# Decoder block on one core: the order of the first four loads, and of the first operations behind them

## The reference

```python
x = x + linear_attention(layernorm(x))       # 16 heads of 16; q, k, v, o projections with biases
x = x + cross(ctx, ctx, masks, layernorm(x)) # see below
x = x + ffn(layernorm(x))                    # Hadamard transforms round gate/up (1024 wide) and down
```

```python
qp = ctx @ Wq.T + bq;  kp = ctx @ Wk.T + bk          # ctx: 4 x 256 x 64
scores = (qp @ kp.T) / 8 * layernorm(x)              # 256 x 256 for each batch
x = x + softmax(where(mask, -inf, scores))
```

## Time and profile before

| | |
|---|---|
| time, median of 3 runs | 125.45 us (125.14, 125.45, 128.5) |
| the profiled execution: its own time | 125.14 us |
| the profiled execution: span from first to last instruction | 123.3 us |
| mean granted clock of TensorE in it | 1.00 of full speed |
| busy share of the span: PE, PEld, DVE, ACT, POOL | 97%, 87%, 67%, 58%, 56% |

### The profile page before, as it was taken

The page is one execution under the profiler, slowest core; times in us unless marked ns, Lnnn a source line. Parts: engine busy times, 40 slices in busy tenths (PEclk is TensorE's granted clock), DMA queues, the critical chain, the costliest instruction groups (busy, mean ns, idle before and its releaser), DMA issues.

```text
span 123.3 us, 2272 instructions
## 1 busy us (share of the span) xinstructions
PE 119.2 (97%) x804; PEld 107.0 (87%) x804; DVE 82.7 (67%) x207; ACT 71.6 (58%) x158; POOL 68.5 (56%) x89
## 2 busy tenths in 40 slices
PE   5999999999999999999999999999999999999990
PEld 2259999999999999999989999988888888889890
DVE  1399989899889899899998959674522332220521
ACT  1785696679748689888491479983135444280000
POOL 2228959979979966959802605762005574066000
DMA  3999910280000000000000110000110000000121
GB/s 123 316 377 423 398 76 5 53 330 3 8 0 0 0 5 3 0 0 0 0 5 0 43 45 0 5 0 0 39 46 3 5 0 0 0 0 0 54 73 43
DMA packets 3823, 7.64 MB, mean 62 GB/s; under 512 B 544, under 2 KB 1952, under 8 KB 3684
## 3 DMA queue, kind: packets, MB, share of 16 engines
q1 hardware_dynamic: 3806, 7.50, 16.8%
q10 hardware_dynamic: 6, 0.01, 0.0%
HBM read 6.46 MB, written 1.05 MB: 61 GB/s over the span
## 4 chain that ended last, share of the span: by engine, by line
PE 97%; POOL 0%; DVE 0%; issue 0%; POOLq 0%
PE bank L1283 19%; PE bank L1295 18%; PE bank L1300 11%; PE bank L1177 10%; PE bank L1304 5%; PE bank L1201 5%; PE bank L1239 5%; PE bank L1155 4%; PE bank L1115 4%; PE bank L1211 3%; PE bank L1221 3%; PE bank L1309 2%; PE bank L1146 2%; PE bank L1247 2%; PE bank L1128 1%; PE bank L1259 1%
## 5 line engine op out<-in xcount | busy, mean ns | idle before, releaser
L1283 PE MATMUL bank<-xh_home,wug 128*128 128x256 f32 x192 | 24.7, 285 | 0.0
L1283 PEld LDWEIGHTS bank<-xh_home,wug 128*128 128x128 f32 x192 | 23.6, 191 | 0.1
L1295 PE MATMUL bank<-xh_home,wug 128*128 128x512 f32 x96 | 22.0, 390 | 0.0
L1295 PEld LDWEIGHTS bank<-xh_home,wug 128*128 128x128 f32 x96 | 18.0, 188 | 3.7
L969 DVE SCALAR_TENSOR_TENSOR back<-bank,sc_up,back 128x512 f32<-128x512 f32 x8 | 6.0, 751 | 15.0 <-PE bank L1295 15.0
L351 POOL TENSOR_TENSOR hs<-back,hs 128x256 fp32r<-128x256 f32 x8 | 5.9, 740 | 17.0 <-ACT hs L614 16.9
L345 POOL TENSOR_TENSOR hs<-front,hs 128x256 fp32r<-128x256 f32 x16 | 11.5, 740 | 6.6 <-ACT hs L599 6.6
L1177 PE MATMUL bank<-watt,xT 128*128 128x256 f32 x96 | 14.0, 288 | 0.0
L1177 PEld LDWEIGHTS bank<-watt,xT 128*128 128x128 f32 x96 | 12.3, 189 | 0.9 <-ACT xT L492 0.7
L606 ACT ACTIVATE back<-bank,vecs 128x512 f32<-128x512 f32 x8 | 5.5, 688 | 12.1 <-PE bank L1295 12.1
L1300 PE MATMUL bank<-wdh,hs 128*128 128x512 f32 x48 | 12.5, 396 | 0.0
(11 more groups left out here) (132 smaller groups left out, 257.6 us busy)
## 6 DMA issues: line engine op xcount, KB each, us to landing
wd_a<-in_w_d SPq DMA_DIRECT2D x1, 1024.0 KB, 8.0
front<-in_w_ug SPq DMA_DIRECT2D x2, 512.0 KB, 8.5
back<-in_w_ug SPq DMA_DIRECT2D x2, 512.0 KB, 3.8
out<-x_res SPq DMA_DIRECT2D x8, 128.0 KB, 1.9
wd_b<-in_w_qkv SPq DMA_DIRECT2D x3, 256.0 KB, 4.5
x_res<-in_x SPq DMA_DIRECT2D x1, 512.0 KB, 6.0
x_res<-in_x_first SPq DMA_DIRECT2D x1, 385.0 KB, 3.1
back<-in_ctx_t SPq DMA_DIRECT2D x1, 260.0 KB
```

Source lines behind the costliest of these rows:

```text
L1283: ins = mm(dst[:, n * SEQ:(n + 1) * SEQ], wug[:, wa, k, at_col + j * P:at_col + (j + 1) * P], xh[b][:, xb, k, :], start=(i == 0), stop=(i ...
L1295: ins = mm(dst[:, :].rearrange("p (b s) -> p b s", s=SEQ), wug[:, wa, k, at_col + j * P:at_col + (j + 1) * P], xh_home[:, PAIR, cols], sta ...
```

## The change

The first load is cut in two: x of batch 0 alone goes first (256 KB), and the unit matrix with the small weights is a load of its own behind it (129 KB). The context comes third and K's weights fourth; the loads behind them keep their order. All bytes stay the same; there is one load more.

On ScalarE, `mx_copy` and `one_rows` come ahead of the high part of K's weights, and `xT_hi(0)` comes ahead of the high part of V's weights and of Q's biases. On VectorE, `xT_lo(0)` comes ahead of `w_lo(1)`, the low part of V's weights. TensorE's list is the same; its first product waits for the new load.

```diff
-        loads = "x0 x1 x2 cst wk wv wq ctx ...
+        loads = "x0 unit x1 x2 cst wk wv wq ctx ...
...
-            sp.dma_start(first[:, 0:X_AT + ST * HID], x_first).then_inc(ld["x0"], 16)
+            sp.dma_start(xs[:, 0:ST, :], x[0]).then_inc(ld["x0"], 16)
+            sp.dma_start(first[:, 0:X_AT], unit).then_inc(ld["unit"], 16)
+            sp.dma_start(ctxT, ctx_t).then_inc(ld["ctx"], 16)
             sp.dma_start(qkv_raw[:, 0], w_qkv[0]).then_inc(ld["wk"], 16)
-            sp.dma_start(ctxT, ctx_t).then_inc(ld["ctx"], 16)
             sp.dma_start(qkv_raw[:, 1], w_qkv[1]).then_inc(ld["wv"], 16)
-            sp.dma_start(xs[:, ST:2 * ST, :], x[0]).then_inc(ld["x1"], 16)
+            sp.dma_start(xs[:, ST:2 * ST, :], x[1]).then_inc(ld["x1"], 16)
...
-            w_hi('wk', 0)
             mx_copy()
             one_rows()
+            w_hi('wk', 0)
             bias_hi(K_COLS)
+            xT_hi(0)
+            w_hi('wv', 1)
             bias_hi(Q_COLS)
-            w_hi('wv', 1)
-            xT_hi(0)
             u_hi(0)
             w_hi('wq', 2)
             u_hi(1)
...
             normalise1(0)
             w_lo(0)
             bias_lo(0, K_COLS)
+            xT_lo(0)
             w_lo(1)
-            xT_lo(0)
             ln_stats(1, 1)
             bias_lo(1, Q_COLS)
             w_lo(2)
...
             def weights_product(_):
                 dst = take("mx", 0)
-                pe.wait_ge(ld["x0"], 16)
+                pe.wait_ge(ld["unit"], 16)
```

More of the change, by code:

```diff
@@ L94, in schedule, with decoder_kernel @@
     return [g for g in order if g not in (("SC", 0, 0), ("SC", 1, 0))]
-def decoder_kernel(nc, x_first, x, ctx_t, w_qkv, bias, w_o, w_ug, w_d, vec, row, row_wsd, mask, const, out):
+def decoder_kernel(nc, unit, x, ctx_t, w_qkv, bias, w_o, w_ug, w_d, vec, row, row_wsd, mask, const, out):
     bank_of, turn_of = {}, {}
@@ L220, in wait_read @@
             eng.wait_ge(read[bank_of[name, i, t]], turn_of[name, i, t] + 1)
-        loads = "x0 x1 x2 cst wk wv wq ctx bias vec row wsd mask wo wd ug0 ug1 ug2 ug3".split()
+        loads = "x0 unit x1 x2 cst wk wv wq ctx bias vec row wsd mask wo wd ug0 ug1 ug2 ug3".split()
         ld = {n: sem("ld_" + n) for n in loads}
@@ L248, in _ @@
             sp.dma_start(cst[:, :], const).then_inc(ld["cst"], 16)
-            sp.dma_start(xs[:, 2 * ST:, :].rearrange("p (b i) d -> p b (i d)", b=BATCH - 2), x[1:].rearrange("b p i d -> p b (i d)")).then_inc(ld["x2"], 16)
+            sp.dma_start(xs[:, 2 * ST:, :].rearrange("p (b i) d -> p b (i d)", b=BATCH - 2), x[2:].rearrange("b p i d -> p b (i d)")).then_inc(ld["x2"], 16)
             sp.dma_start(wd_a[:, :, :], w_d).then_inc(ld["wd"], 16)
@@ L1410 @@
     arrays = {
-        "x_first": np.concatenate([np.eye(P, dtype=np.float32), w_x, blocks(a["x"][0]).reshape(P, -1)], 1),
-        "x": np.stack([blocks(a["x"][b]) for b in range(1, BATCH)]),
+        "unit": np.concatenate([np.eye(P, dtype=np.float32), w_x], 1),
+        "x": np.stack([blocks(a["x"][b]) for b in range(BATCH)]),
         "ctx_t": np.concatenate([a["ctx_512"].reshape(TOK, CTX).T, np.ones((1, TOK), np.float32)]),
```

## The result

The changed kernel is slower: its runs against the runs of before have the ratio 1.0121 (95% interval 1.009 to 1.0151), some 1.5 us, with a median of 126.88 us (126.28 to 127.63 in four runs). That lies above the range of the prediction, 124.9 to 126.3. Some executions of most kernels here, of before too (128.5 and 128.73 of its four), come out some per cent longer; they are left out of every ratio and range in this document, and the plain medians (before: 126.97) can't be set side by side. Beside the experiments, 81 more runs of the kernel before were timed; 52 of them stand between 125.1 and 125.8.

The account below looks back on a forecast made before the run. TensorE, busy 119.2 of 123.3 us, was taken as the bound. Loads and ScalarE's order cost 0, VectorE's order +0.2: 125.35 from the profiled 125.14, 125.65 from the median, middle 125.5; range 124.9 to 126.3.

Parts of the forecast that it names:

- The loads: Head of the kernel: one more load issued by SP delays no load, since bytes are the same; cost 0.
- The other bound, 0.42: SP's issuing: the extra load could cost 0.42 us on a late load; the forecast took 0.
- K's weights land when the context did, at the latest 6.15: Head loads: K's weights, now fourth, land between near 5.3 and 6.15 us; cost 0.
- the 0.59 us of cover: ScalarE: work on K's weights and biases ends at 7.13 us, 0.59 ahead of `xT_hi` at 7.72; cost 0.
- `u` 0 stands behind the warm-up: TensorE's head: the warm-up holds `u` 0, so an earlier context can't help.
- Rival (d): Head: a gain beyond 0.1 us, needing TensorE to have waited for x or the context; chance 0.05.
- VectorE's order: `w_lo(1)` behind `xT_lo` makes VectorE 0.57 us later; TensorE pays 0.2 once, at `T1` 1.
- just in time: Q's first product: `w_lo(2)` is ready at 11.74 us against the weight load at 11.73; cost 0.01.
- the extra 0.4 us of x's slack: Ahead of `T1` 0: x lands 0.38 us earlier, slack grows from 0.38 to 0.76; gain 0.
- the unit matrix no hindrance: First product `mx`: the unit matrix lands near 3.79 us, at most 4.54, ahead of 4.82; cost 0.
- K 1's start as the end of the matter: TensorE: no further cost at `K` 1; from there on everything is 0.2 us later.
- (c): Head: the unit matrix's own load pays start-up again, `mx` is 1.63 us late, time 126.8; chance 0.03.

Follow-up runs that it names:

- VectorE's order undone: The changed kernel with `w_lo(1)` ahead of `xT_lo(0)` again on VectorE; ratio 1.009 to the kernel before.
- the orders alone: The kernel before, its loads kept, with the new orders on ScalarE and VectorE; ratio 1.0008 to the kernel before.
- the same kernel again: The changed kernel run and profiled once more with no edit; ratio 1.0039 to the kernel before, runs 125.54 to 126.23 us.
- the exchange: The kernel before with the new ScalarE and VectorE orders, first load whole, context second, K's weights third; ratio 0.9998 to the kernel before.
- the useless load: The kernel before with a 32 KB load that nobody waits for, second in SP's row; ratio 1.0123, two runs, 126.31 and 127.7 us.
- the cut alone: The changed kernel with K's weights third and the context fourth again, first load still cut; ratio 1.0248 to the kernel before.

## Why the prediction was wrong

**The step that failed** is in "The loads": "loads queue for bandwidth, not for SP, and the bytes are the same. I take 0". A load more in SP's row had a price though the bytes were the same: 0.95 us ahead of `T1` 0 in the profiled execution, the masks 1.53 later, and ratios of 1.004 to 1.025 in the kernels that have it, against 0.9975 with the same loads and one fewer in the row. The other bound, 0.42, was too small as well. The step rested on K's weights being in 3.4 us after their issue. That they wait long doesn't show what they wait for, nor that every part of a load comes at the rate of its bytes. Bytes did set when most parts came: all of the context but one part by 5.03, 13 of the 16 parts of K's weights by 5.93. The context counted as in with its last part (7.01), and the last parts were up to two microseconds behind the others.

The busy share of the DMA engines would not have decided it. From 3.2 to 5.6 us it is 0.96 in the first profile of before, 0.74 in the second, and 0.88 in the changed kernel.

**With it failed** "K's weights land when the context did, at the latest 6.15": 7.49 in the changed kernel, 6.00 with the first load whole. In the changed kernel this cost nothing on top, because `T1` 0 was late itself; of the 0.59 us of cover, 0.24 were left ahead of `xT_hi` (its idle time, ended by the transposes). In the run with VectorE's order undone the context was in time, the cover was used up, and TensorE waited for `xT_hi`.

**A reading that was half the truth:** "`u` 0 stands behind the warm-up". So it does when the warm-up runs at its slower pace (1.03 us for its last two products): with the context in earlier, `u` 0 starts at 6.06 (the orders alone, the same kernel again). But the context landed at 6.01 in the first profile of before, so the slack was about 0: in the changed kernel, with the context 1.00 us later (7.01), `u` 0 came 0.99 late, and in the second profile of before `u` 0 waits until 6.67. Rival (d) could win 0.1 us by an earlier context, and up to 0.4 only in an execution whose warm-up is faster.

**Right in mechanism, wrong in size:** VectorE's order. It is paid between Q 0 and `T1` 1 and nowhere after (SC 0, ST 0 and K 1 are 1.37, 1.38 and 1.38 late), by `w_lo(2)` and by the normalisation behind the mean, as the steps said. I put 0.2 us; it is 0.41 in the changed kernel, 0.46 with the orders alone, 0.62 with the exchange. Q's "just in time" was a wait of 0.20, and Q's first six products then took 0.98 us in place of 0.88, which the sum left out. With nothing lost at the loads the forecast would thus still have been short by half, +0.2 for 0.41.

**Right:** `bn_stats` at 3.38, `mx` at 4.82, the extra 0.4 us of x's slack of no use, the unit matrix no hindrance, and K 1's start as the end of the matter.

**The rivals.** (c) had the load of its own as the culprit, but neither the way nor the place: the unit matrix landed at 3.65, 0.29 behind x, `mx` stood at 4.82, and no start-up was paid again. That its 126.8 lies next to the median of 126.88 is luck. The 0.95 us of the profile came from one part of the context. The row that the prediction set against (c), K's weights 0.75 us behind the first load, was read rightly; what it can't show is a single part that falls behind.

**What stays open.** Why packets are held up for one or two microseconds when one load more stands in the row is not shown, nor whether it is the length of the row or the time of issue that counts. The trace shows that it is single packets, and that a part that has fallen behind stays behind; which DMA engine moved which part isn't recorded here. The loss also isn't the same in each execution (125.54 to 127.63 for the changed kernel), it doesn't grow with a second cut, and which load is late varies.

## What to carry to other kernels

At the head of a kernel count the loads in an issuing engine's row before counting bytes: here a load cut in two made the first half 0.4 us early and loads behind it late (`u` 0 at 7.14 for 6.15, the masks at 9.99 for 8.46), unless another engine issued the second half (`u` 0 at 5.86). Before giving a load a landing time, read it from more than one profile, and look at its last part: here the bytes told when most of it came (13 of the 16 parts of K's weights by 5.93, the last at 7.47). And look for an operation that runs in time in which its engine would have waited: `w_lo(1)` was free there, cost 0.41 to 0.62 us moved behind the wait (3.96 to 4.17 us from V 0 to SC 0, 3.55 before), and none of it on GpSimd, which idled then (3.55).

## What the runs showed of the hardware that was not expected

- One load more, of 32 KB, second in SP's row: `u` 0 at 7.18 us (6.15 and 6.67 in two profiles of the kernel before), the masks taken up at 10.53 (8.46 and 8.91).
- In the changed kernel, one packet of 4 KB took 2.15 us where the median is 0.16, and the last part of each load behind it landed 1.6 to 2.0 us after the middle one, down to the masks.
- An idle time of TensorE of 1.91 us ahead of `u` 0 was followed by a granted clock of 0.55 from 8 to 12 us, one of 1.58 us (the useless load) by 0.50; in the changed kernel, one of 1.06 us was followed by 1.00. In the run with the cut alone I take that for a part of its 2.5%: the mean granted clock of its four runs is 0.973 to 0.997.
- The context's landing varied by half a microsecond between two profiles of one kernel (`u` 0 at 6.15 and 6.67 in the kernel before), so a step with no slack in one profile had a cost in the next.
